# The order of VectorE's work in the first attention, its output bias on GpSimd, and identity products in TensorE's waits

## What is computed

```
x = x + L0_xattn(layernorm(x), ctx, ...)   # 16 heads of 16; 48 main keys and 16 "dca" keys per row, two softmaxes; @ Wo + bo
x = x + L0_ffn(layernorm(x), ...)          # silu gate, 768 wide, weights rounded to e4m3
x = x + L1_xattn(layernorm(x), ctx, ...)   # 16 heads of 128, rmsnorm on q and k
x = x + L1_ffn(layernorm(x), ...)          # gelu gate, 1024 wide, e4m3 operands
```

## Time and profile before

| | |
|---|---|
| runs shown, median | 737.57 us (734.79 to 739.28) |
| the profiled execution | 737.14 us, of which 735.3 us are the span and 1.84 us lie around it |
| TensorE busy | 678.7 us, 92% of the span |
| VectorE busy | 548.8 us, 75% |
| ScalarE busy | 481.2 us, 65% |
| GpSimd busy | 431.2 us, 59% |
| mean granted clock of TensorE | 0.976 |
| first attention | from the start to about 184 us |
| last down products | about 724.8 to 729.7 us |

### The profile page before, as it was taken

How to read it: one execution, slowest core, us unless ns; L and a number is a source line. 1 busy time by engine, 2 the same in 40 slices (tenths; PEclk the granted TensorE clock), 3 DMA queues, 4 the chain that set the end, 5 groups by cost and what they waited for, 6 DMA issues and landing times.

```text
span 735.3 us, 16270 instructions
## 1 busy us (share of the span) xinstructions
PE 678.7 (92%) x5814; PEld 539.5 (73%) x5814; DVE 548.8 (75%) x1180; ACT 481.2 (65%) x982; POOL 431.2 (59%) x635
## 2 busy tenths in 40 slices
PE   2889999987999989999999999999999999999784
PEld 1567767655888877888888888888888888876442
DVE  3699999986488886768677676676676766766887
ACT  1478777663556667666666666666666666668994
POOL 2487787774677735665656656656666654464600
PEclk9999999986999999999999999999999999999996
DMA  8200001300310000000000000100000000000001
GB/s 284 68 9 9 10 9 56 126 2 1 129 59 29 8 16 1 15 24 16 15 29 10 21 24 11 32 12 23 23 16 9 22 1 2 2 1 1 30 29 58
DMA packets 26019, 22.83 MB, mean 31 GB/s; under 512 B 5041, under 2 KB 24402, under 8 KB 25810
## 3 DMA queue, kind: packets, MB, share of 16 engines
q1 hardware_dynamic: 24160, 20.92, 8.9%
q10 hardware_dynamic: 1778, 0.86, 0.4%
HBM read 19.67 MB, written 2.10 MB: 30 GB/s over the span
## 4 chain that ended last, share of the span: by engine, by line
POOL 36%; issue 25%; DVE 17%; PE 17%; ACT 3%; ACTq 1%; POOLq 1%; DVEq 0%
POOL rstd L683 14%; POOL pr L651 5%; POOL p_n L658 5%; PE banks L1478 3%; PE banks L1499 3%; PE banks L1500 3%; POOL w L674 2%; POOL w_raw L671 2%; DVE prob L790 2%; DVE h_sum L1017 2%; DVE hid_b L1010 1%; POOL var L681 1%; DVE smax L786 1%; POOL prob L621 1%; DVE ssum L816 1%
## 5 line engine op out<-in xcount | busy, mean ns | idle before, releaser
L683 POOL TENSOR_TENSOR rstd<-var,minus_half 128x8 f32<-128x8 f32 x64 | 106.1, 1657 | 5.0
L658 POOL TENSOR_TENSOR p_n<-pr,pinv 128x256 f32<-128x256 f32 x64 | 39.3, 613 | 75.7 <-DVE pinv L925 75.7
L651 POOL TENSOR_TENSOR pr<-pr,rstd 128x256 f32<-128x256 f32 x63 | 38.6, 613 | 74.1 <-DVE pr L935 74.0
L1205 ACT ACTIVATE kT<-banks,gk_q 128x512 f32<-128x512 f32 x64 | 44.0, 688 | 49.1 <-PE banks L1601 49.1
L1591 PE MATMUL banks<-m_hi,z_hi 128*128 128x256 f32 x256 | 74.9, 293 | 0.7 <-DVE z_lo L916 0.6
L1591 PE MATMUL banks<-m_hi,z_lo 128*128 128x256 f32 x256 | 72.3, 283 | 0.0
L1591 PE MATMUL banks<-m_lo,z_hi 128*128 128x256 f32 x256 | 72.3, 282 | 0.0
L916 DVE TENSOR_TENSOR z_lo<-banks,z_hi 128x512 fp32r<-128x512 f32 x64 | 43.8, 685 | 29.1 <-ACT z_hi L1190 29.0
L963 DVE TENSOR_REDUCE sums<-q_sq 128x4 f32<-128x512 f32 x64 | 43.7, 682 | 25.3 <-ACT q_sq L1229 25.2
L1251 ACT ACTIVATE qT<-banks 128x512 f32<-128x512 f32 x64 | 38.2, 597 | 32.9 <-PE banks L1695 32.9
L931 DVE TENSOR_REDUCE pmax<-banks 128x4 f32<-128x256 f32 x64 | 27.0, 421 | 41.2 <-PE banks L1622 41.1
(11 more groups left out here) (194 smaller groups left out, 2095.0 us busy)
## 6 DMA issues: line engine op xcount, KB each, us to landing
w_raw<-in_L_xattn_Wq SPq DMA_DIRECT2D x4, 512.0 KB, 5.7
wo_raw<-in_L_xattn_Wo SPq DMA_DIRECT2D x1, 2048.0 KB, 8.3
k_ctx<-in_ctx SPq DMA_DIRECT2D x16, 128.0 KB, 2.7
w_raw<-in_L_ffn_w_gating SPq DMA_DIRECT2D x16, 128.0 KB, 2.4
out_x<-x_sb SPq DMA_DIRECT2D x4, 512.0 KB, 3.1
x_sb<-in_x SPq DMA_DIRECT2D x1, 1536.0 KB, 9.2
a_ctx<-in_ctx SPq DMA_DIRECT2D x16, 64.0 KB, 1.8
w_raw<-in_L_xattn_Wk SPq DMA_DIRECT2D x2, 512.0 KB, 9.4
```

The source lines that it names most:

```text
L651: pool.tensor_tensor(pr[:, u % 2, :, :], pr[:, u % 2, :, :], roots_of[:, HC:2 * HC].unsqueeze(2).to_broadcast([P, HC, S]), ALU.mult).then_ ...
L658: pool.tensor_tensor(p_n[:, u % 2, :, :], pr[:, u % 2, :, :], pinv[:, u % 2, :].unsqueeze(2).to_broadcast([P, HC, S]), ALU.mult).then_inc( ...
L683: pool.tensor_tensor(rstd1[:, par, :], var1[:, :], minus_half[:, :].to_broadcast([P, 2 * HC]), ALU.pow).then_inc(root1, 1)
L1205: act.activation(kT[u % 2][:, :, :].rearrange("p h n -> p (h n)"), bank[2][:, :], ACT.Copy, scale=gk_q[:, :]).then_inc(kT_ready, 1)
```

## The change

In VectorE's step the addition to `x` and its moments (tile i-2) move up, between the sum of squares and the first guess; the weight chunk's two rounding instructions move down, to just before the sums of the exponentials. In ScalarE's step the square of tile i+2 moves up, to right after the exponential. The product that began each output with the bias is dropped, with its row of ones; instead GpSimd adds the bias to `x` of tile i-1, after its rounding of the weight chunk and before the division, and VectorE waits for that before it adds the output. TensorE gets products of the identity with itself whose results nobody reads: 11 before its first work, 4 ahead of the queries and keys of tiles 0, 1 and 2, 4 ahead of the turning of tiles 0 and 1, and 6 ahead of three of the last four down products.

```diff
@@ pool (GpSimd)
-            pool.memset(ones_row[0:1, :], 1.0).then_inc(ones_set, 1)
@@ pool, step: after the chunk's rounding, before the division
+                t = i - 1
+                if live(t, NT):
+                    if t == 0:
+                        pool.wait_ge(bo_ready, 1)
+                    pool.wait_ge(xhat_ready, t + 1)
+                    pool.tensor_tensor(x_sb[:, t, :], x_sb[:, t, :], bo_bc[:, :], ALU.add).then_inc(x_biased, 1)
@@ dve (VectorE), step
                     dve.tensor_reduce(half2[:, t % 2, :, 0], qk_sq[:, :, :], AX.X, ALU.add).then_inc(ln_steps, 1)
+                t = i - 2
+                if live(t, NT):
+                    dve.wait_ge(y_done, t + 1)
+                    dve.wait_ge(x_biased, t + 1)
+                    dve.tensor_tensor(x_sb[:, t, :], y_bank(t)[:, 0:D], x_sb[:, t, :], ALU.add).then_inc(x_updated, 1)
+                    dve.wait_ge(x_updated, t + 1)
+                    dve.bn_stats(row_bn[:, t, :], x_sb[:, t, :]).then_inc(row_steps, 1)
+                    moments(dve, 1, t, 1)
+                t = i + 1
+                if live(t, NT):
                     dve.wait_ge(ln_steps, LN_N * t + 1)
                     first_guess(...)
-                for c in chunks(i):                     # e4m3_magic, moved down
...
-                t = i - 2                               # the addition and moments, moved up
...
                     dve.tensor_tensor(qk_cent[...], bank[1][:, :], bqk[...], ALU.add).then_inc(cent_ready, 1)
+                for c in chunks(i):
+                    if c == 0:
+                        dve.wait_ge(w0_in, 3 * 16)
+                    after(dve, w0_steps, 2 * (c - 1))
+                    e4m3_magic(dve, magic_steps, 2 * c, w0_raw[:, c * W_CHUNK:(c + 1) * W_CHUNK], rnd2[:, c % 2, :, 0])
@@ act (ScalarE), step: moved from before turned_keys to after the exponential
+                t = i + 2
+                if live(t, NT):
+                    act.wait_ge(cent_ready, t + 1)
+                    after(act, ln_steps, LN_N * (t - 1) + 1)
+                    act.activation(qk_sq[:, :, 0:HD0], qk_cent[:, t % 2, :, :], ACT.Square, scale=SQ_SCALE).then_inc(sq_ready, 1)
@@ pe (TensorE)
+            def keep_busy(n, to):
+                for _ in range(n):
+                    nc.tensor.matmul(to[:, 0:P], ident[:, :], ident[:, :], start=True, stop=True)
+            pe.wait_ge(centred, 3)
+            keep_busy(11, bank[2])
...
+                    if t < 3:                           # ahead of queries and keys, t = i + 2
+                        keep_busy(4, bank[2])
                     pe.wait_ge(xT_ready, 3 * (t + 1))
...
+                    if t < 2:                           # ahead of the turning, t = i + 1
+                        keep_busy(4, bank[2])
                     pe.wait_ge(scaled, t + 1)
...
-                    if t == 0:
-                        pe.wait_ge(bo_ready, 1)
-                        pe.wait_ge(ones_set, 1)
+                    pe.wait_ge(o_evac, t + 1)
                     after(pe, x_updated, t)
-                    nc.tensor.matmul(y_bank(t)[:, 0:D], ones_row[0:1, :], bo_bc[0:1, :], start=True, stop=False)
-                    pe.wait_ge(o_evac, t + 1)
                     for kk in range(KD):
-                        last = nc.tensor.matmul(..., start=False, stop=kk == KD - 1)
+                        last = nc.tensor.matmul(..., start=kk == 0, stop=kk == KD - 1)
...
             for u in range(ND - 4, ND):
+                if u != ND - 3:
+                    keep_busy(6, bank[6])
                 down8(u)
```

More of the change, by code:

```diff
@@ L225, in build @@
         prm = sb(sa, "prm", [P, D])
-        ones_row = sb(sa, "ones_row", [P, P])
+        b_room = sb(sa, "b_room", [P, 128])
         a_cT = sb(sa, "a_cT", [P, 2, 2, PER, S])
@@ L323, in build @@
         o_done, o_evac, y_done = sem("o_done"), sem("o_evac"), sem("y_done")
-        ones_set, x_updated = sem("ones_set"), sem("x_updated")
+        x_biased, x_updated = sem("x_biased"), sem("x_updated")
         stored = sem("stored")
@@ L770, in step @@
                     dve.tensor_reduce(half2[:, t % 2, :, 0], qk_sq[:, :, :], AX.X, ALU.add).then_inc(ln_steps, 1)
+                t = i - 2
[8 more added lines that the diff above has]
+                if live(t, NT):
                     dve.wait_ge(ln_steps, LN_N * t + 1)
                     first_guess(dve, LN_N * t + 1, half2[:, t % 2, :, 0], rstd2[:, t % 2, :, 0], qk_tmp[:, t % 2, :])
-                for c in chunks(i):
[L775 to L778, removed]
                 t = i
@@ L791, in step @@
                                           smax[:, seg, :].unsqueeze(2).to_broadcast([P, H, hi - lo]), ALU.subtract).then_inc(shifted, 1)
-                t = i - 2
[L793 to L799, removed]
                 t = i + 2
@@ L1129, in step @@
                                    scale=cols[:, 0, 0:1], bias=cols[:, 0, 1:2]).then_inc(t_evac, 1)
[L1130 to L1134, removed]
                 t = i + 1
@@ L1425, in step @@
                 if live(t, NT):
-                    if t == 0:
-                        pe.wait_ge(bo_ready, 1)
-                        pe.wait_ge(ones_set, 1)
+                    pe.wait_ge(o_evac, t + 1)
                     after(pe, x_updated, t)
-                    nc.tensor.matmul(y_bank(t)[:, 0:D], ones_row[0:1, :], bo_bc[0:1, :], start=True, stop=False)
-                    pe.wait_ge(o_evac, t + 1)
                     for kk in range(KD):
-                        last = nc.tensor.matmul(y_bank(t)[:, 0:D], oT[:, kk, :], wo0[:, kk, :], start=False, stop=kk == KD - 1)
+                        last = nc.tensor.matmul(y_bank(t)[:, 0:D], oT[:, kk, :], wo0[:, kk, :], start=kk == 0, stop=kk == KD - 1)
                     last.then_inc(y_done, 1)
```

## The result

The changed kernel took **733.78 us** (median of 6 runs, 733.12 to 735.25), the kernel before on the same chip 737.23 us. The ratio is **0.9956, with a 95% interval of 0.9935 to 0.9976**: about 3.3 us faster, within 1%. The forecast was 736.5 us. The profiled execution took 733.76 us, with a span of 732.0 us against 735.3.

What follows compares the result with a forecast made beforehand. VectorE was taken to set the 8.88 us a tile, part of it stalls beside GpSimd. The terms +1.2 +0.5 +0 -0.5 -1.5 -0.3 = -0.6 on the profiled 737.14 gave 736.5 us, range 731 to 740.5.

Steps and rivals of the forecast that it cites:

- the forecast's own case: Whole kernel: the summed terms hold, 736.5 us with a range of 734 to 740; chance 0.58.
- first steps +0.5: Steps 0 and 1: GpSimd's queue runs longer than VectorE's, +0.5 us once, bounds 0 and 1.5.
- The turned order moves the stall: Steady tiles: stall goes from L412 to the chunk's two instructions, period 8.97 us against 8.88, +1.2 us over 13 tiles.
- held until N+8.2: L412, timed from GpSimd's refinement start N: arrives 0.5 us before GpSimd's L621 ends and waits for that end.
- rival 3: Steady tiles: L431 misses a 0.07 us gap and is held for L615 too, 0.75 us a tile, 746 us; chance 0.04.
- Bias on GpSimd, hidden: Steady tiles: GpSimd's added instruction, 0.73 us, fits its idle time with 0.2 us to spare and costs nothing.
- Products in the head, -0.5 at tile 2: First tiles: products raise TensorE's clock, first scores 1 to 1.5 us sooner; -0.5 us at tile 2, bounds -2 and +2.
- No fall of the clock in the middle, -1.5: At 144 to 148 us: TensorE's idle time is spread out, so the clock stays up; -1.5 us, bounds 0 and +1.5.
- The drain, 0: Drain of the pipeline after 160 us: it keeps its waits, 0 us.
- Last products, -0.3: Last down products: six products raise the clock, last four records about 0.5 us; -0.3 us, bounds -0.5 and +3.
- Rival 1: Steady tiles: the chunk is not held, GpSimd bounds, period 8.62 us, -3.4 in place of +1.2, 732 us; chance 0.22.
- Rival 2: Head and drain: the head's first clock fall and one of the drain's go too, 2 to 3 us more, 734 us; chance 0.10.

Runs made afterwards that it cites:

- e3: Changed kernel with the weight chunk's two rounding instructions put back right after the first guess; 730.93 us, 0.9907 of the kernel before.
- e10: Changed kernel with one more GpSimd addition of 128x128 per tile, its result unused; 735.87 us, 0.9956 of the kernel before.
- e5: Kernel before with only the output bias moved to GpSimd, old order, no identity products; 735.43 us, ratio 0.9978.
- e1: Kernel before with all the identity products added, order and bias as before; 738.08 us against 738.50, ratio 0.9996.
- e2: Changed kernel without any identity product; 733.92 us, 0.9948 of the kernel before.
- e8: Changed kernel without the first tiles' identity products, those ahead of the last down products kept; 733.00 us, 0.9937 of the kernel before.
- e7: e3 without the first tiles' identity products, those ahead of the last down products kept; 730.66 us, 0.9908 of the kernel before.
- e6: Kernel before with only the turned order on VectorE and ScalarE, bias on TensorE, no identity products; 737.77 us, ratio 1.0010.
- e4: Changed kernel with the output bias back on TensorE, new order and products kept; 736.52 us, 0.9983 of the kernel before.

## Why the prediction was right

**Right in the total, and partly by luck.** The time lay in the range of 731 to 740.5, on the side forecast, within 1%. It lay 0.2 us below the 734 to 740 of the forecast's own case. The sum had -0.6 us against the profiled execution before, and the profiles differ by 3.3. By stretches: up to tile 3 forecast 0 (head -0.5, first steps +0.5), found -0.15; tiles 3 to 14 forecast -0.3 (+1.2 -1.5), found -0.95; the drain forecast 0, found -2.05; the rest of the program -0.3, found -0.15. Most of the gain lies where the forecast had none. One reading was loose, without effect: the third share of the chain, 11.7%, is "issue" and not VectorE's. By its steps:

1. *The turned order moves the stall.* Right, and shown: L429 0.89 us and L431 0.71 (0.6 or more was asked for), the period hardly moved, and e3 without the collision has 8.48. The term was off by 0.10 us a tile: +1.2 us in the sum, where the period of 8.87 makes -0.1. With N = 94.08 (L418's start and 0.27), L412 arrives at N+7.66, for the N+7.68 forecast, but L627 then is not in one piece: its second begins at N+7.68. The step that failed is the one that has L412 "held until N+8.2". It goes through between the pieces, which I had written down as possible in rival 3 and not put into the sum. The hold falls on L414 and ends at N+8.34, a little later than forecast, with two instructions behind it instead of three, so L418 starts at N+8.60, not N+8.7.
2. *Bias on GpSimd, hidden.* Right in the steady tiles: 0.74 us for the 0.73 taken, 0.29 us of idle time left for the 0.2 worked out, and e10's 0.46 us on top cost 0.08. Wrong in one word, "nothing", for the roots of steps 7 and 11: 112.10 - 102.80 = 9.30 us, 0.43 over the period, about the 0.5 us named there, and 0.31 at step 11. In the old order it is not given back either: e5 takes 9.14 us for the step that the kernel before does in 8.88. The first steps cost more than the +0.5 and less than its bound: from tile 1's maxima to tile 3's it is 18.1 us in the kernel before and 17.9 in e1, 19.1 in e2 and 19.2 in e8, all four at the full clock. That is of order and bias together.
3. *Products in the head, -0.5 at tile 2.* The clock is up at 16 us, as forecast. That this brings the first scores 1 to 1.5 us sooner failed, though the changed kernel's profile shows 1.2. In the six profiles with products in the head the first maxima come at 29.3, 30.8, 31.4, 31.5, 31.7 and 31.8 us, in the eight without at 30.2 to 32.1. What I had not seen is that TensorE then waits for tile 2's input. That turning starts between 23.2 and 23.9 us in all six, with idle times of 1.46 us (changed kernel, at 23.41) to 2.8 ahead of it; it needs a transfer of context that the SP queue issues at 20.49 us, behind those of the scales (13.00 and 15.40). A higher clock before it only makes the wait longer, and after the longer waits the clock is down again (0.50 in e1's row). In time e1, e7 and e8 show nothing gained.
4. *No fall of the clock in the middle, -1.5.* In the profile it came true: 1.00 from 60 to 158 us, where the kernel before spends 10.44 us between the maxima at 138.54 and 148.98. But e1, with the old order and the old bias, has no such fall either, and it does tiles 3 to 14 in 97.8 us, the changed kernel in 98.35. So without a fall on either side the changed kernel is 0.6 us slower there, by the roots' steps. Whether the change makes falls rarer is open. The mean granted clock over whole runs, which does not say where the falls lie, is 0.973 for the kernel before and 0.979 for both e1 and e2 on one chip, and 0.976 for the kernel before, 0.982 for e5 and 0.976 for e6 on another. I took one execution's fall for a property of the kernel.
5. *The drain, 0.* This is the largest miss. From tile 14's maxima to the next network the kernel before takes 184.05 - 157.87 = 26.2 us, the changed one 24.1. The product with the row of ones was in the drain too; I had costed its removal at nothing, for the steady tiles, and then carried the zero over to where TensorE is the one that is waited for. One link shows its price: 0.63 us at 182.64. The profiles of the other runs, put side by side by order and by clock, give the whole (us):

| from tile 14's maxima to the next network | product on TensorE | bias on GpSimd |
|---|---|---|
| old order, clock down by 164 us | 26.2 (before), 26.5 (e1) | 24.6 (e5) |
| turned order, clock down by 164 us | 26.1 (e4) | 24.1 (changed) |
| turned order, clock up until 170 us or later | 23.2 (e6) | 21.1 (e2), 22.0 (e8), 21.2 (e10) |

The product costs 1.2 to 2.1 us at like clock, as much as the stretch gained. A clock that stays up is worth 2 to 3 us more, but the two profiles of the main comparison both have it down by 162 us, so it is no part of their difference. These are single profiles. e2's row, with the clock up:

```profile
158.00:174.00 16.00, 8.60 (x140) 6.25 (x140) 14.12 (x29) 7.48 (x15) 11.32 (x20) 1.00 0.00 1
```

6. *Last products, -0.3.* Right: 0.26 us between e8 and e2 (six products took 1.50 us for the 1.3 worked out, the last group 0.60 for 0.5), and down to nothing where the clock is up anyway.

Rival 1 priced the chunk without the hold at a period of 8.62 us and 732 us, with GpSimd as the bound. It was no description of this kernel, but nearly of e3: 8.48 us and 730.9, with the bound elsewhere. Rival 2's time, 734, is the closest to the measured one. Its mechanism is not what the profile shows: the fall at 32 us is gone, but there is one at 54 instead, and the drain keeps its falls.

## What to carry to other kernels

Where a small instruction on VectorE takes several times its usual length, look for the GpSimd instruction whose end it shares; moving it is worth something only if the place it goes to, or the work that takes its place, meets no such instruction. Here it was beside GpSimd's short instructions that the chunk was not held. A wait inside the loop that sets the period is no spare time, and an engine without idle time need not be the bound: take work from it and look whether the period moves. And cost a removed instruction in the drain of a pipeline by itself: what is free in the steady tiles may be waited for at the end.

## What the runs showed that I had not expected

An instruction that comes just between two pieces of a GpSimd operation passes at its full speed: L412 took 0.15 us at 101.74, with L627's second piece starting at 101.76, and 0.98 us where it came to the middle of the first piece, at 100.53 in the kernel before. The Trainium skill (SBUF — State Buffer, Who interferes with whom) says that whichever of the two engines issues first gets the shared pair for the whole instruction. L627's two pieces are two instructions, and this agrees.

TensorE's clock falls at different places in executions of nearly the same program: in single profiles it is down at 144 us (before), 54 us (changed), 58 to 66 us (e10), and nowhere between 36 and 174 us (e2). A term of 1.5 us read from one profile's fall can't be counted on.
